# Head attention with exponentials of three banks: two places of three banks for scores, a ring of 18 banks for probabilities

## The reference

```python
x = x + _L0_attn_a_ref(_layernorm(x, axis=-1))   # 16 heads of 16, q = k = v = the normalised x
x = x + _L0_ffn_ref(_layernorm(x, axis=-1), ...)
x = x + _L0_attn_b_ref(_layernorm(x, axis=-1), ...)
x = x + _L0_ffn_ref(_layernorm(x, axis=-1), ...)
```

```python
qkv = x.reshape(B, S, H, hd).transpose(0, 2, 1, 3)
q = k = v = qkv
w = jnp.einsum('bhqd,bhkd->bhqk', q, k) / jnp.sqrt(jnp.asarray(hd, x.dtype))
w = jnp.where(causal[None, None, :, :], w, mask_value)
w = jax.nn.softmax(w, axis=-1)
out = jnp.einsum('bhqk,bhkd->bhqd', w, v)
```

## Time and profile before

| what | value |
|---|---|
| median of 3 runs | 1744.38 us (1744.1 to 1744.78) |
| the profiled execution | 1745.11 us, span 1743.4 us |
| PE busy | 1683.6 us, 97% of the span |
| ACT busy | 952.8 us, 55% |
| DVE busy | 1015.4 us, 58% |
| exponentials L556 | 544, first start 17.2 us, last start 526.1 us |

### The profile page before, as it was taken

The page is one execution under the profiler, slowest core; times in us unless marked ns, Lnnn a source line. Parts: engine busy times, 40 slices in busy tenths (PEclk is TensorE's granted clock), DMA queues, the critical chain, the costliest instruction groups (busy, mean ns, idle before and its releaser), DMA issues.

```text
span 1743.4 us, 27922 instructions
## 1 busy us (share of the span) xinstructions
PE 1683.6 (97%) x10527; PEld 1152.8 (66%) x10527; DVE 1015.4 (58%) x2116; ACT 952.8 (55%) x1260; POOL 305.0 (17%) x402
## 2 busy tenths in 40 slices
PE   6999999999999999999999999999999999999998
PEld 2222222222227888888878888889888888888886
DVE  5352233344328765865556677766897876575554
ACT  6999999999995222422235444554444432242221
POOL 2112212212200000000015335534443100000000
PEclk9999999999999999999999999999999999999999
DMA  4100100000120020000000000000000200300000
GB/s 134 25 13 14 25 19 13 20 19 15 45 71 1 1 88 10 1 0 1 0 1 1 1 1 1 1 1 1 1 1 25 73 1 12 113 10 13 13 12 24
DMA packets 33681, 35.91 MB, mean 21 GB/s; under 512 B 3255, under 2 KB 30478, under 8 KB 33550
## 3 DMA queue, kind: packets, MB, share of 16 engines
q1 hardware_dynamic: 33550, 34.14, 6.6%
HBM read 22.07 MB, written 4.19 MB: 15 GB/s over the span
## 4 chain that ended last, share of the span: by engine, by line
PE 69%; ACT 14%; issue 10%; DVE 5%; POOL 0%; DMA 0%; ACTq 0%; SPq 0%; DVEq 0%
ACT a_probs L556 14%; PE f_h L794 7%; PE f_h L796 7%; PE f_h L795 7%; PE f_ypsum L796 7%; PE f_ypsum L794 7%; PE f_ypsum L795 7%; PE d_outs L794 4%; PE d_outs L795 4%; PE d_outs L796 4%; PE d_banks L794 3%; PE d_banks L796 3%; PE d_banks L795 3%; PE a_out L662 2%; PE a_scores L691 2%
## 5 line engine op out<-in xcount | busy, mean ns | idle before, releaser
L556 ACT ACTIVATE a_probs<-a_scores 128x1024 f32<-128x1024 f32 x544 | 502.0, 1159 | 8.5 <-PE a_scores L691 7.7
L1124 ACT ACTIVATE f_gelu<-f_h,f_bcol 128x512 f32<-128x512 f32 x256 | 176.6, 690 | 468.8 <-PE f_h L796 465.6
L662 PE MATMUL a_out<-a_probs,a_values 128*32 128x512 f32 (+3 forms) x2560 | 294.3, 541 | 12.0 <-ACT a_probs L556 8.8
L1179 DVE TENSOR_SCALAR f_hh<-f_gelu,f_gates 128x512 fp32r<-128x512 f32 x256 | 124.8, 488 | 236.9 <-ACT f_gelu L1124 235.7
L1611 ACT ACTIVATE d_score<-d_dist,d_nksq 128x512 f32<-128x512 f32 x128 | 92.8, 725 | 222.2 <-DVE d_dist L1754 220.4
L1181 DVE SCALAR_TENSOR_TENSOR f_hl<-f_gelu,f_gates,f_hh 128x512 fp32r<-128x512 f32 x256 | 192.4, 752 | 9.2
L691 PE MATMUL a_scores<-a_moving,a_fixed 64*128 64x512 f16 (+3 forms) x1280 | 184.5, 352 | 13.2 <-ACT a_probs L556 4.5
L691 PEld LDWEIGHTS a_scores<-a_moving,a_fixed 64*128 64x128 f16 x1280 | 47.0, 94 | 207.0 <-ACT a_probs L556 168.3
L1648 POOL TENSOR_TENSOR distance_raw<-distance_raw,d_p 128x512 f32<-128x512 f32 x112 | 146.1, 1305 | 198.5 <-ACT d_p L1586 198.3
L570 POOL TENSOR_SCALAR_AFFINE_SELECT a_probs<-a_probs 128x256 f32<-128x256 f32 (+1 forms) x224 | 97.6, 450 | 427.6 <-ACT a_probs L556 426.5
L794 PE MATMUL f_h<-c_xhi,f_w 128*128 128x512 f32 x384 | 155.0, 404 | 0.0
(11 more groups left out here) (228 smaller groups left out, 2876.9 us busy)
## 6 DMA issues: line engine op xcount, KB each, us to landing
f_raw<-in_L_ffn_W SPq DMA_DIRECT2D x24, 512.0 KB, 7.6
a_fixed<-a_moving SPq DMA_DIRECT2D x60, 96.0 KB, 2.3
out<-x SPq DMA_DIRECT2D x8, 512.0 KB, 2.9
x<-in_L_attn_a_x SPq DMA_DIRECT2D x7, 512.0 KB, 8.2
f_raw<-in_L_ffn_W SPq DMA_DIRECT2D x12, 256.0 KB, 3.6
a_fixed<-a_moving SPq DMA_DIRECT2D x60, 32.0 KB, 2.0
f_early_raw<-in_L_ffn_W SPq DMA_DIRECT2D x4, 256.0 KB, 3.4
x<-in_L_attn_a_x SPq DMA_DIRECT2D x2, 256.0 KB, 3.0
```

The source lines that it names most:

```text
L556: act.activation(probs[:, u % UR], scores[:, 2 * (u % SR):2 * (u % SR) + 2, :], ACT.Exp, scale=HD ** -0.5)\
L662: mm = pe.matmul(spare[32 * j:32 * j + 32, i % 2, skip:skip + w], values[:, G % 2, kt + tile, j, :], probs[:, u % UR, j % 2, col:col + w], ...
L1124: act.activation(gel[:, n % HR, :], hps[:, n % 2, :], ACT.Gelu, bias=mix.bcol[:, q, FT * e + j:FT * e + j + 1])\
L1179: dve.tensor_scalar(hh[:, n % HR, :], gel[:, n % HR, :], gate, None, ALU.mult).then_inc(s_hh, 1)
```

## The change

An exponential no longer takes a unit of two banks but three banks in sequence (EB = 3), across the borders of units and steps. `scores` keeps its six banks, now two places of three, and `probs` becomes a ring of PR = 18 banks (16 before). `split_f`, needed only at the start, is placed over the last two banks of that ring. PE waits, at each third bank, for the exponential two before (`bank // EB - 1` finished ones); it counts `s_scores` up for every bank, and fills a step's banks one after the other: in `pair` and `last` steps the two matmuls of one half come before the two of the other half. The products wait for as many exponentials as cover their step (`exps`), the masks likewise.

```diff
@@ -301,14 +301,16 @@
-        split_f = sb("a_split_f", [P, 2, TPC, GH, 4, HD], F16)
         split_m = sb("a_split_m", [P, 2, TPC, GH, 2, 2, HD], F16)
-        UR, SR = 8, 3
-        probs = sb("a_probs", [P, UR, 2, CHUNK], F32)
+        EB, SR, PR = 3, 6, 18
+        ring = pr.place()
+        probs = sb("a_probs", [P, PR, CHUNK], F32)
+
+        split_f = pr.over("a_split_f", [P, 2, TPC, GH, 4, HD], F16, ring + (PR - 2) * CHUNK * 4)
...
-        scores = ps("a_scores", [P, 2 * SR, CHUNK], F32)
+        scores = ps("a_scores", [P, SR, CHUNK], F32)
@@ -334,8 +336,16 @@
-        units = [(n, i) for n, (G, c, kind, kt) in enumerate(steps) for i in range(UNITS[kind])]
-        first_unit = [units.index((n, 0)) for n in range(len(steps))] + [len(units)]
+        first_bank, step_of = [0], []
+        for n, (G, c, kind, kt) in enumerate(steps):
+            first_bank.append(first_bank[-1] + 2 * UNITS[kind])
+            step_of += [n] * (2 * UNITS[kind])
+        banks = len(step_of)
+
+        def exps(n):
+
+            return -(-first_bank[n] // EB)
@@ -547,14 +557,16 @@
-            for u in range(len(units)):
-                if u == first_unit[GS * (NG - 1) + 6]:
+            for u in range(-(-banks // EB)):
+                if u == first_bank[GS * (NG - 1) + 6] // EB:
                     mix.tanh(act, 0, routing)
-                act.wait_ge(s_scores, u + 1)
-                if u >= UR:
-                    act.wait_ge(s_pv, units[u - UR][0] + 1)
-                act.activation(probs[:, u % UR], scores[:, 2 * (u % SR):2 * (u % SR) + 2, :], ACT.Exp, scale=HD ** -0.5)\
-                   .then_inc(s_exp, 1)
+                last = min(EB * (u + 1), banks)
+                wide = last - EB * u
+                act.wait_ge(s_scores, last)
+                if last > PR:
+                    act.wait_ge(s_pv, step_of[last - 1 - PR] + 1)
+                act.activation(probs[:, EB * u % PR:EB * u % PR + wide, :], scores[:, EB * u % SR:EB * u % SR + wide, :], ACT.Exp,
+                               scale=HD ** -0.5).then_inc(s_exp, 1)
@@ -562,9 +574,9 @@
-                    for u in range(first_unit[n], first_unit[n + 1]):
-                        pool.wait_ge(s_exp, u + 1)
-                        blocks = probs[:, u % UR].rearrange("p h (q n) -> p (h q) n", n=P)
+                    for bank in range(first_bank[n], first_bank[n + 1], 2):
+                        pool.wait_ge(s_exp, (bank + 1) // EB + 1)
+                        blocks = probs[:, bank % PR:bank % PR + 2, :].rearrange("p h (q n) -> p (h q) n", n=P)
@@ -654,13 +666,13 @@
-                pe.wait_ge(s_exp, first_unit[n + 1])
+                pe.wait_ge(s_exp, exps(n + 1))
...
@@ -678,17 +690,16 @@
-                for u in range(first_unit[n], first_unit[n + 1]):
-                    if u >= SR:
-                        pe.wait_ge(s_exp, u - SR + 1)
+                for bank in range(first_bank[n], first_bank[n + 1]):
+                    unit, h = divmod(bank - first_bank[n], 2)
+                    head = slice(64 * h, 64 * h + 64)
+                    if bank >= SR and (bank % EB == 0 or bank == first_bank[n]):
+                        pe.wait_ge(s_exp, bank // EB - 1)
                     for tile, skip, w, unit_of, col_of in pieces[kind]:
                         q0, k0 = c * CHUNK + skip, (kt + tile) * P
                         for a in range(2):
-                            if first_unit[n] + unit_of[a] != u:
-                                continue
-                            for h in range(2):
-                                head = slice(64 * h, 64 * h + 64)
-                                mm = pe.matmul(scores[:, 2 * (u % SR) + h, col_of[a]:col_of[a] + w], fixed[G % 2][head, a, k0:k0 + P],
+                            if unit_of[a] == unit:
+                                mm = pe.matmul(scores[:, bank % SR, col_of[a]:col_of[a] + w], fixed[G % 2][head, a, k0:k0 + P],
                                                moving[G % 2][head, a, q0:q0 + w], start=True, stop=True)
                     mm.then_inc(s_scores, 1)
```

More of the change, by code:

```diff
@@ L660, in products @@
                     for j in range(GH):
-                        u, col = first_unit[n] + unit_of[j // 2], col_of[j // 2]
+                        bank, col = first_bank[n] + 2 * unit_of[j // 2] + j % 2, col_of[j // 2]
                         mm = pe.matmul(spare[32 * j:32 * j + 32, i % 2, skip:skip + w], values[:, G % 2, kt + tile, j, :],
-                                       probs[:, u % UR, j % 2, col:col + w], start=(kt == 0 and kind in ("full", "first")),
+                                       probs[:, bank % PR, col:col + w], start=(kt == 0 and kind in ("full", "first")),
                                        stop=(kind == "last"), skip_group_check=True)
```

## The result

The changed kernel takes 1844.26 us (median of 4 runs, 1839.81 to 1844.36), the kernel before 1744.24 us beside it (1743.04 to 1744.78). The ratio is 1.0565, 95% interval 1.0553 to 1.0578: slower by 100 us, where 1842 us and slower were forecast.

A forecast was written before the change was run, and what follows sets the result against it. ACT, with next to no slack, bounds the attention before the change. Then 69.2 + 3.1 + 1.2 + 1.7 = 75.2 us a group; 8 x 75.2 + 4.9 = 606.5 against 508.9, +97.6, so 1842 us; 8-in-10 range 1792 to 1872.

The forecast's parts named there:

- The exponential: ACT in the head attention: 1536 elements last 1.45 us, 1.33 us start to start; 8.6 us saved if never waiting.
- The loop: Round trip through PE and ACT in full attention steps: 6.11 us for 12 banks, where exponentials before took 5.42.
- Its four steps: Exponential's end to next start 1.80 us, next starts 1.53 and 1.33 us later, then the last exponential's 1.45 us.
- The sum: Attention group of 136 banks: bare loop plus three extras, 75.2 us against 63.0; +97.6 us over the whole kernel.
- bare loop: Full-step round trip without the extras, 0.509 us per bank: 69.2 us for a group's 136 banks.
- transposes: PE's four `turn` and four `turn_out` in a group: 4.6 us of work, 3.1 counted on the loop.
- order of matmuls by halves: In `pair` and `last` steps, same-half matmuls no longer start together: 1.8 us a group, 1.2 counted.
- masks: Products of `pair` units wait for mask selects, some 0.85 us; half counted, four times: 1.7 us a group.
- Idle ACT before the exponentials: ACT waiting for scores in the profile after: some 120 us in all, where it was 7.7.
- were covered until now: Other work in PE's order, such as transposes, was hidden before the change; now two thirds of it counts.
- The faster one: Rival: two places suffice and ACT stays the bound with fewer fixed costs; -8.6 us, 1736 us; chance 0.08.
- The lower clock: Rival: PE's clock falls from 2.4 to 1.2 GHz in the attention; 32 us a group, about 2100 us; chance 0.04.

The follow-up runs named there:

- the doubled ones: Four transposes of each finished output made twice: 1850.8 us in the changed kernel; in the kernel before, 1753.58 us, ratio 1.0050.
- The kernel with alternating halves: Changed kernel with the two halves' matmuls of pair and last steps alternating again wherever a unit's two banks lie in one place: 1843.77 us.
- the kernel before with the lag alone: Kernel before with products three steps behind the scores in place of two, nothing else moved: 1761.71 us, ratio 1.0100.

## Why the prediction was right

**The exponential.** 1.45 us long, 1.33 or 1.35 us from start to start where none waits (1.34 in the mean): both as priced, within 0.01 us. By these starts the saving would be 4 to 5 us, an estimate from 544 x 0.903 - 363 x 1.34, and not 8.6; no run shows it, since it is buried under stalls.

**The loop.** Its four steps measure 1.83, 1.50, 1.34 and 1.45 us, against 1.80, 1.53, 1.33 and 1.45. What makes it was told apart by two kernels: two places without products inside them cost 50 us, and the same two places of three with the products moved out of them give 70 of 100 us back. So a turn with only one place ahead costs time by itself, and the group of products within the place makes most of the 100 us. Products inside a place with a third place of three banks ahead were not tried; nine banks and the two of `spare` are more than the eight of PSUM. For the rule of the Trainium skill that rotating through different PSUM banks lets evacuation and matmuls overlap (Perfetto Trace Analysis, Optimizing Tensor Performance), the runs add a condition: the change rotates, and ACT still waited 138 times.

**The sum.** 75.2 us a group were forecast, 74.9 measured. By its terms:

| term, us a group | forecast | measured |
|---|---|---|
| bare loop, all banks | 69.2 | 70.6, as what the other rows leave |
| transposes, 4.6 us of work | 3.1 | 2.8, if all pay like the doubled ones (0.60) |
| order of matmuls by halves | 1.2 | 0, with two units of three put back |
| masks | 1.7 | 1.5 |

So one term was wrong, the order by halves: priced by columns and counted on the path, it costs nothing where it was tried. What stands in its place, 1.4 us more than the bare loop, was not tried by itself. The first and last group together were given 4.9 us more than eight groups; 603.4 - 8 x 74.9 leaves 4.2. That the sum comes within 0.3 us a group is in part luck: the order's 1.2 us too much and the 1.4 us that no row accounts for cancel. Two slips in the arithmetic are too small to matter: 4 x (0.55 + 0.58) is 4.5 us and not 4.6, and 544 x 0.903 - 363 x 1.33 is 8.4 and not 8.6.

**Other steps.** Idle ACT before the exponentials was forecast at 120 us and reads 93.6. That was a slip between two bases: from start to start the stalls are 603.4 - 363 x 1.33 = 121 us, but an idle time begins at the end of a 1.45 us record. For the same reason ACT is busy 84% and not 80% of a group. That the transposes "were covered until now" was wrong: doubled, they cost the kernel before 1.2 us a group and the change 1.4. The sum did not rest on it, since it was made from the changed kernel's own loop.

**The rivals.** The faster one fell with the 1.83 us in the trace. The lower clock came true in small: see below. It may be the cause of the 4.5 us between the profiled execution and the median.

## What to carry to other kernels

Before an evacuation is made wider at the cost of a place, work out the turn: from the release of a place, through everything that the producer's fixed order has ahead of the last matmul into it, to the next start. If that is longer than what the consumer still has ahead, the stall comes each time, whatever either engine's busy share says. When sizes no longer divide each other (three banks, four a step), foreign work slips inside a place; moving it behind the place gave back more here than any other change of the order. And a lag is not a number on its own: what is timed against it has to move along.

## What the runs showed of the hardware

The granted clock of TensorE fell within the attention, which it did not in the kernel before. In the changed kernel it fell once in the profiled execution, here in stretches as in the earlier trace rows, then PE and ACT in order of time:

```profile
473.00:478.30 5.30, 3.95 (x42) 1.39 (x39) 1.76 (x4) 4.06 (x3) 1.17 (x3) 1.00 0.01 3
478.30:481.70 3.40, 3.16 (x13) 0.43 (x13) 0.00 (x0) 1.69 (x3) 0.00 (x0) 0.55 0.00 0
```

```profile
479.00 1.94 PE L674 MATMUL a_out<-a_probs,a_values 128*32 128x512 f32 x8
...
481.54 1.45 ACT L568 ACTIVATE a_probs<-a_scores 128x1536 f32<-128x1536 f32 x1 [1.71 <-PE a_scores L702]
```

PE had worked 3.95 of 5.3 us before it, less than its 64 of 75. For some 3.4 us the clock was at its lower level, 1.2 GHz; the products took 1.94 us and not 1.07, and ACT waited 1.71 us. The kernel with alternating halves had three such falls in its trace, two of them in groups 3 and 4, which took 79.5 and 75.9 us where the change without a fall took 78.0 and 74.3: 1.5 us for each. The changed kernel's other three runs have a mean granted clock of 0.994 or 0.995 against the profiled one's 0.998 and are 4.5 us longer. An estimate from these figures: 0.003 to 0.004 of 1842 us is 6 to 7 us of clock, or three to four more falls of 3.4 us to half, 1.5 us each; no trace of these runs shows them.

Three banks are not needed for it. In the kernel before with the lag alone the clock fell twice, at 29.9 us for 3.4 us and at 439.5 us for 6.8 us, both next to PE's two longest waits for DVE behind the start (3.13 and 2.49 us): PE had been busy 0.27 of 3.4 us and 1.01 of 2.5 us just before. Its six waits of 1.98 us had no fall beside them. The kernels with two places of two and with products behind a place had none in their traces. So in the kernels in which PE waits long or in each loop, the time can hold a little more than the waits.
